# q's fp16 halves made two tiles ahead, and the scaling of v's state moved from VectorE to ScalarE, in a gated slot attention kernel

## The reference

```
ge = exp(f_t)
hk = hk * ge[:, :, None, :] + k_t[..., :, None] * s_t[..., None, :]
logits = einsum('bhk,bhkm->bhm', q_t * scale, hk)
p = softmax(logits)
hv = hv * ge[..., :, None] + s_t[..., :, None] * v_t[..., None, :]
o_t = einsum('bhm,bhmv->bhv', p, hv)
```

## Time and profile before

| what | us |
|---|---|
| median of three runs | 3056.42 |
| profiled execution | 3053.13 |
| its span, first to last instruction | 3051.4 |
| PE busy over the span | 2910.8 (95%) |
| DVE busy | 2669.0 (87%) |
| POOL busy | 2043.7 (67%) |
| ACT busy | 1854.0 (61%) |

### The profile page before, as it was taken

The page is one execution under the profiler, slowest core; times in us unless marked ns, Lnnn a source line. Parts: engine busy times, 40 slices in busy tenths (PEclk is TensorE's granted clock), DMA queues, the critical chain, the costliest instruction groups (busy, mean ns, idle before and its releaser), DMA issues. The chain is left out here.

```text
span 3051.4 us, 102767 instructions
## 1 busy us (share of the span) xinstructions
PE 2910.8 (95%) x34624; PEld 2557.7 (84%) x34624; DVE 2669.0 (87%) x4370; ACT 1854.0 (61%) x5448; POOL 2043.7 (67%) x3191
## 2 busy tenths in 40 slices
PE   5999999999999999788999999998899999999999
PEld 4888888888888888678888888888788888888888
DVE  7999999999999998477888888887899999999998
ACT  2777777777777777767777777776222222222222
POOL 5788888888888887356666666666555555555553
PEclk9999999999999999899999999999999999999999
DMA  4455555555555555456666666665333333333332
GB/s 107 114 138 138 137 137 138 137 138 137 137 138 137 137 138 134 155 142 167 179 175 175 177 179 175 175 179 149 89 77 76 76 76 76 76 76 76 76 76 58
DMA packets 814248, 387.11 MB, mean 127 GB/s; under 512 B 586068, under 2 KB 748244, under 8 KB 814168
## 3 DMA queue, kind: packets, MB, share of 16 engines
q1 hardware_dynamic: 814168, 386.07, 49.0%
HBM read 184.49 MB, written 134.22 MB: 104 GB/s over the span
## 5 line engine op out<-in xcount | busy, mean ns | idle before, releaser
L777 PE MATMUL banks<-ffn_xT_hl,w_hl 128*128 128x128 f16 x12288 | 729.7, 219 | 0.0
L499 PE MATMUL banks<-w_hl,midT_hl 128*128 128x256 f16 x6144 | 712.5, 273 | 6.6 <-DVE low_hl L696 6.0
L777 PEld LDWEIGHTS banks<-ffn_xT_hl,w_hl 128*128 128x128 f16 x12288 | 704.2, 98 | 3.9 <-issue 0.6
L499 PEld LDWEIGHTS banks<-w_hl,midT_hl 128*128 128x128 f16 x6144 | 595.4, 98 | 75.7 <-DVE midT_hl L690 7.8
L669 DVE TENSOR_TENSOR_SCAN runmax<-restart,banks 128x1024 f32<-128x1024 f32 x256 | 585.6, 2287 | 8.1 <-PE banks L756 0.2
L608 ACT ACTIVATE midT_hl<-banks 128x1024 f16<-128x1024 f32 x256 | 262.1, 1024 | 300.8 <-PE banks L789 300.8
L690 DVE SCALAR_TENSOR_TENSOR midT_hl<-banks,midT_hl 128x1024 f16<-128x1024 f32 x256 | 312.0, 1219 | 90.9 <-ACT midT_hl L608 90.9
L298 POOL TENSOR_TENSOR ffn_xT_hl<-ffn_xT,ffn_xT_hl 128x256 f16<-128x256 f32 x256 | 190.0, 742 | 279.6 <-ACT ffn_xT_hl L293 277.0
L674 DVE TENSOR_TENSOR step<-runmax 128x1024 bf16<-128x1024 f32 x256 | 338.8, 1323 | 8.9
L499 PE MATMUL banks<-wqkfv_hl,att_xT_hl 128*128 128x512 f16 (+1 forms) x1536 | 293.7, 328 | 2.0 <-issue 1.4
L614 ACT ACTIVATE low_hl<-banks 128x128 f16<-128x128 f32 x256 | 70.3, 275 | 352.8 <-PE banks L499 352.8
(11 more groups left out here) (141 smaller groups left out, 6826.5 us busy)
## 6 DMA issues: line engine op xcount, KB each, us to landing
projected<-qkvf_out SPq DMA_DIRECT2D x128, 384.0 KB, 2.4
ffn_xT<-ffn_blocks SPq DMA_DIRECT2D x1024, 32.0 KB, 2.0
gates_d<-gates_out SPq DMA_DIRECT2D x128, 256.0 KB, 2.8
gates<-gates_d SPq DMA_DIRECT2D x128, 256.0 KB, 3.7
qkv<-projected SPq DMA_DIRECT2D x128, 256.0 KB, 2.8
x_in<-in_L_attn_x SPq DMA_DIRECT2D x128, 128.0 KB, 2.6
x_res<-in_L_attn_x SPq DMA_DIRECT2D x128, 128.0 KB, 2.3
x<-x_out SPq DMA_DIRECT2D x128, 128.0 KB, 2.2
```

The source lines that it names most:

```text
L499: last = nc.tensor.matmul(dst, left(lp, k), right(rp, k), start=(k == 0 and lp == rp), stop=(k == blocks - 1 and lp == 1))
L777: nc.tensor.matmul(mid_ps[t.slot][:, cols], w1_hl[:, wp, k, cols], xT_hl[:, t.ring, xp, k], start=(c % PER_BANK == 0 and k == 0 and wp == xp),
```

## The change

Two edits. `q_high` and `q_low` work for tile t+2 in step t (before: t+1), and stand later in their queues: on ACT behind `softmax_exp`, on POOL behind `weight`. `decay_Hv` leaves DVE; on ACT it copies the four diagonal 64x64 blocks of `state_sum` with a scale per partition. The off-diagonal blocks of v's state are zeroed once, by a memset on DVE ahead of the first `make_St`. Because `decay_Hv` of chunk 3 now reads `state_sum` on another engine, `add_states` of the next chunk 0 waits for it.

```diff
@@ on_gpsimd
-                return Phase([(q_low, 1), (rms, -2), (weight, 0), (own_decay, 2), (o_low, -4)],
+                return Phase([(rms, -2), (weight, 0), (q_low, 2), (own_decay, 2), (o_low, -4)],
@@ on_scalar
+                def decay_Hv(t):
+
+                    if isinstance(t.n, int) and t.n == 0:
+                        act.wait_ge(S["state_cleared"], 1)
+                    if t.chunk:
+                        after_chunk(act, S["decay_col_made"], t, LATER)
+                        after_chunk(act, S["state_sum_made"], t, EARLIER, lag=1)
+                        after(act, S["o_done"], t, lag=2)
+                        for a in range(PAIRS):
+                            for z in range(2):
+                                rows = slice(z * HD, (z + 1) * HD)
+                                last = nc.scalar.activation(state[rows, t.slot, 1, a, rows],
+                                                            state_sum[rows, 1, a, rows], ACT.Copy,
+                                                            scale=decay_col[rows, t.ring, a:a + 1])
+                        last.then_inc(S["Hv_made"], 1)
-                return Phase([(q_high, 1), (evacuate_PtT, -1), (evacuate_T, 1), (square_sums, -2),
-                               (softmax_exp, 0), (o_high, -4), (exp_sums, 2)],
+                return Phase([(evacuate_PtT, -1), (evacuate_T, 1), (square_sums, -2),
+                               (decay_Hv, 0), (softmax_exp, 0), (q_high, 2), (o_high, -4), (exp_sums, 2)],
@@ on_vector
                 def make_St(t):
-
+                    if isinstance(t.n, int) and t.n == 0:
+                        nc.vector.memset(state[:, :, 1], 0.0).then_inc(S["state_cleared"], 1)
...
                     else:
+                        after_chunk(dve, S["Hv_made"], t, LATER, lag=1)
                         nc.vector.tensor_copy(state_sum[:, :, :, :], update).then_inc(S["state_sum_made"], 1)
...
-                def decay_Hv(t):
-
-                    if t.chunk:
-                        after_chunk(dve, S["decay_col_made"], t, LATER)
-                        after_chunk(dve, S["state_sum_made"], t, EARLIER, lag=1)
-                        after(dve, S["o_done"], t, lag=2)
-                        for a in range(PAIRS):
-                            last = nc.vector.scalar_tensor_tensor(
-                                state[:, t.slot, 1, a], state_sum[:, 1, a], decay_col[:, t.ring, a:a + 1],
-                                own_head[:, :], ALU.mult, ALU.mult)
-                        last.then_inc(S["Hv_made"], 1)
-                return Phase([(divide_o, -2), (decay_Hv, 0), (k_low, 1), (scale_logits, 0),
+                return Phase([(divide_o, -2), (k_low, 1), (scale_logits, 0),
                                (mask_AB, 1, 2), (finish, -5), (add_states, 0), (make_St, 2), (decay_Hk, 1),
                                (invert_totals, 0), (turn_o, -3)],
```

More of the change, by code:

```diff
@@ L1383, in build @@
             "inv_total_made", "Pt_made", "PtT_done", "PtT_made",
-            "update_done", "state_sum_made", "Hk_made", "Hv_made",
+            "update_done", "state_sum_made", "Hk_made", "Hv_made", "state_cleared",
             "o_done", "o_raw_made", "o_sum_made", "o_sum_eps_made", "o_rms_made",
```

## The result

The changed kernel takes 3098.07 us in the median of four runs (3095.80 to 3104.12), beside 3055.4 us for the kernel before: 1.0141 times, 95% interval 1.0128 to 1.0155. The forecast was 3011 us, faster with a chance of 0.93. It was wrong in sign, and all three of its signs of being wrong came: a sequence above 25 us, small copies followed later than 0.26 us, and new idle time before PE's transposes. The profiled execution took 3095.80 us with a span of 3094.0 us, 42.6 us more than before.

What follows compares the result with a forecast made beforehand. PE's waits before products_A were taken as the bound; afterwards PE (24.1 + 0.4), ACT (24.3) and DMA (24.4 us) nearly tie. At 24.65 us, 1.38 saved over 31 sequences gives 43 us off 3053.1: forecast 3011 us, range 2997 to 3032.

Steps and rivals of the forecast that it cites:

- What bounds the kernel before: PE in the attention loses 1.94 us of a 26.03 us sequence, nearly all before products_A, mostly waiting for k_low behind decay_Hv.
- the 1.45 that the sum gave: PE's waits before products_A removed per sequence of four steps: 0.78 + 0.45 + 0.05 + 0.17 = 1.45 us.
- decay_Hv on ACT, 0.24 us each: Four small copies a step in chunks 1 to 3, 0.96 us a step, between 0.56 and 1.04, within ACT's wait for the softmax.
- third rival: decay_Hv on ACT holds the softmax; old time reached at 0.385 us a copy, 3096 us at 0.5; chance 0.03.
- ACT as a loop: ACT's way round one step takes 4.57 + 1.55 = 6.12 us, as close as 0.1 us to setting the pace.
- St at 0.43 us: Term in ACT's way round a step: St, between expnG and the transposes, keeps 0.43 us.
- q two tiles ahead, a gain of 0.17 us: q_low comes a step early and is never late; chunk 0's products_A starts at 1616.04 instead of 1616.21.
- The way through the DMA: From expnG through St and the block moves to the next expnG: 6.16 us a step, 24.4 us a sequence.

Runs made afterwards that it cites:

- hv_behind_logits: Kernel before with decay_Hv kept on DVE but moved from ahead of k_low to behind scale_logits, q unchanged: 3024.80 us, ratio 0.9910.
- hv_on_act_alone: Kernel before with only the scaling of v's state moved to ACT, q one tile ahead at the head of the step as before: 3070.98 us, ratio 1.0049.

## Why the prediction was wrong, by its own steps

*What bounds the kernel before: right.* products_A waited for k_low, not for q_low as the rows name it. The one entry moved in `hv_behind_logits` takes 1.03 us of the 1.45 that the sum gave, with q untouched.

*decay_Hv on ACT, 0.24 us each: this is the step that failed first.* The copies took 0.36 us, 1.44 us a step instead of 0.96. The forecast read the pace of short instructions from the square's row to the row of its accumulator read, 0.14 us on, and from the exponential's to its own, 0.26. But the next ACTIVATE came 0.24 and 0.34 us on, the instruction's own duration: the read is hidden in it. The earlier trace rows had both (1602.53 to 1602.77; 1604.73 and four in 1.35 us), and the true upper bound was 0.34, from which the forecast's own third rival, slower above 0.385, was near. The Trainium skill's figures ("ScalarE: Activation LUTs", section "What ACT_TABLE_LOAD costs") fit the durations, 0.34 us with a per-partition operand and 0.25 without, and nearly the 93 ns between them (0.343 against 0.254 us in the median); the overlap of 93 ns between neighbours, which made 239 ns of it, did not show here between these 64-column copies (0.36 and 0.27 us apart).

*ACT as a loop: right in kind, mis-sized, and by more than the copies.* With 0.36 us a copy the sum of 6.12 us becomes 6.6 us a step, some 25.8 us a sequence: that alone would still be a little faster than before. The way round ACT measured above is 7.19 us. Against the forecast's terms the copies add 0.47 us, the way from kT_hl to the squares 0.33 (0.60 instead of 0.27, since it waits for o_raw behind the long Hk), and St 0.20 (0.63 instead of 0.43); the rest is small and partly cancels. So the second step that failed is St at 0.43 us, and with it Hk and o_raw: what q_low runs beside was put at nothing without a reason. The copies on ACT with q as before cost 0.49 us a sequence against having them on DVE.

*q two tiles ahead, a gain of 0.17 us: right in sign by itself (0.32 us measured), wrong beside the copies.* The sum of gains has no cost for it, though the sum of ACT's loop does count q_high, at 0.39 us (it took 0.31). In its old place q_high filled a time in which ACT would have waited for PE's transposes anyway (with it there, 28.3 us of that wait were left in 59 steps). In front of the gate exponentials it costs 0.41 us a sequence. And q_low was called never late, with no look at what it then runs beside: 0.88 us a sequence, since St and Hk are held by it and by own_decay and o_low, which it pushes back. The chain 26.02 (before), +0.49 (copies to ACT), +0.41 (q_high), +0.88 (q_low) gives 27.80, each step of it a measured kernel. The shares belong to this order of the steps; in another order they would differ, as the single edits show.

That POOL holds St and Hk is a rule that the forecast should have weighed: the Trainium skill ("SBUF — State Buffer", section "Who interferes with whom") says that a VectorE instruction with two SBUF inputs contends with a GpSimd instruction that reads SBUF, and that the one issued first goes first. The trace agrees for POOL's instructions on 256 columns: St and Hk end 0.28 to 0.29 us after POOL's instruction when that was first. It does not for o_rms, which works on four columns in 1.01 us: in `hv_behind_logits` the two of decay_Hv run beside it and take 0.34 us each, where they took 0.72 in the median before, beside o_low and q_low. Why is open. The rows before the change carried the warning, in decay_Hv's 1.46 us for two.

*The way through the DMA: not reached.* With 24.79 us a sequence in the fastest order the estimate of 24.4 us for it is not contradicted, nor shown.

*The third rival, decay_Hv holding the softmax,* had the right place. Its point of decision, 0.385 us a copy, left out how St and Hk grow beside POOL; 0.36 us was enough for slower even in `hv_on_act_alone`. It had a chance of 0.03, and "no 64-column row on ACT is followed later than 0.26 us" was the misreading of the accumulator rows again.

## What to carry to other kernels

Before work moves into an engine's "idle" time, walk that engine's queue once round the loop with the start-to-start distance of whole neighbours of the same kind, and count twelve small instructions as twelve durations. Moving a stage in a list moves it past neighbours: ask for each what it now runs beside, above all a GpSimd instruction beside a VectorE one with two SBUF inputs. And where a wait is caused by an instruction standing in front of another, try first to let them change places on the same engine: one entry moved gave 0.9%, while the move to another engine lost 0.5%, and 1.4% together with q's.

## What the hardware showed that was not expected

- Four 64x64 copies on ACT with a constant scale follow one another 0.27 us apart, 0.36 us with a scale per partition, each slightly more than its own duration (0.25 and 0.34 us), while the 256-column copies of 0.38 us out of PE's banks follow 0.27 to 0.28 us apart and the 256-column copies of 0.40 us within SBUF 0.30 to 0.31 us apart (1610.09 to 1610.70 after). Which property of the small copies prevents the overlap was not tried.
- On DVE, 64x64 blocks with one input take 0.22 us at best and up to 0.68 us beside POOL, so four cost more than two 128x128 with two inputs and a mask (0.34 us each when no wide POOL instruction runs).
- Which of two goes first decides which is held: before the change POOL's q_low takes 0.85 us where Hk stands 0.10 us ahead of it (1607.97) and 0.67 us elsewhere (1615.48), while that Hk keeps its 0.42 us.
